# Order of the first loads in a pre-norm attention and feed-forward kernel: activation tiles 4 to 6 ahead of the feed-forward factors, and new planned arrival times

## The chip, the cores and the metric

The kernel runs on the 8 cores of one Trainium2 chip. Each core computes one of the 8 batch elements; the cores exchange nothing. The metric is the device time of the slowest core, in microseconds (us).

## The reference

For each batch element, x has 2048 rows (the sequence) of 1024 features:

```
x = x + Attn(layernorm(x));  x = x + FFN(layernorm(x))
Attn: Q, K, V = h@Wq+bq, h@Wk+bk, h@Wv+bv      16 heads of 64
      scores = Q K^T / 8 + decay,  decay = -0.25*log(i-j) for j < i, 0 for j = i, -inf for j > i
      out = softmax(scores) V @ Wo + bo
FFN:  W_real, W_imag (512 x 512) = einsum('abcd,cefg->abefdg', G1, G2)   (from small factors)
      out_real = xr@W_real.T - xi@W_imag.T + b_real;  out_imag = xr@W_imag.T + xi@W_real.T + b_imag
```

## The kernel before

The 2048 rows are 16 tiles of 128 (a tile number n or t) and 4 chunks of 512 (c). Heads go in 8 pairs (p). TensorE works through numbered groups into two alternating PSUM banks `gp`; a group may start when the group two before it has been evicted. The groups are: T(n), the transposes of a normalised tile (PE line L979); K(c,p) and Q(c,p), the projections of a chunk for one pair, 8 matmuls each (L991); V(t,half), values of a tile for eight heads (L1001); N and B, a bound on the scores from the squared norms of Q and K (L1012, L1020); O and F, the output projection and the feed-forward. The attention proper runs in 320 steps: scores (L1055, L1057) on TensorE, the exponential X on ScalarE (L931), the product with the decay P on VectorE (L798), the values and row sums on TensorE (L1079, L1085). The groups of the second half of a chunk and of the next chunk are laid between the attention steps.

The start of chunk 0 has no attention steps beside it. TensorE's order there is T(0) to T(3), K(0,0) to K(0,3), Q(0,0) to Q(0,3), N(0,0), V(0,0), N(0,1), V(1,0), V(2,0), B(0,0), V(3,0), then the scores of the first two steps, K(0,4), Q(0,4), K(0,5) and so on. Pairs 0 to 3 need the first halves of the weights (columns 0 to 511), pairs 4 to 7 the second halves. In chunk 0 ScalarE evicts K and Q; VectorE evicts N and V. Before N(0,0), VectorE squares Q and K of pairs 0 and 1 (L772, L773), before N(0,1) those of pairs 2 and 3.

GpSimd issues all weight loads at the start, in the order Wk, Wq, Wv first halves, then Wk, Wq, Wv second halves (L604, through the software queue q0). SyncE issues the rest (hardware queue q1): tiles 0 to 3 of x, then behind a wait for Wk's first half half of the V bias `bvB` and the selectors, behind a wait for Wq's first half what the change touches. Tiles 4 and later go to three buffers `xrot`; tile 7 and every later one waits in SyncE's queue until the tile that held its buffer is normalised (L578 to L580).

A tile's layer norm on VectorE is two halves of statistics (S1, S2: L653, L660) and the application A (L670); ScalarE computes the reciprocal root R between them. The 56 factor steps W on VectorE (L755, L759) build the feed-forward weight from `g1s` and `g2s`; after each 7 ScalarE rounds the result (WR, L911, L913). The first W step waits for both loads. `g1s` and `g2s` lie where chunk 2's attention output is written later, so the first normalisation of chunk 2 waits for the last rounding.

TensorE's order does not depend on planned times of loads: `make_fill` writes it from costs and due places. The orders of ScalarE and VectorE are written by `make_orders`: it plays the program with a planned duration for each instruction and a planned arrival time for each load (the tasks with `"dma"`), and, whenever one of the two engines is free, takes among the work that is ready by the plan's clock what TensorE needs soonest. At run time each engine follows this order strictly and waits where the real data are late.

Of the kernel before, what the change touches and what calls it, by code (L numbers as in the profile page):

```python
# [71 lines left out]
def on_act(lab):  # L72

    return (lab[0] == "B" or (lab[0] in ("K", "Q") and lab[1] == 0)
            or (lab[0] == "T" and (lab[1] < 4 or lab[1] >= NT + 12)))
# [129 lines left out]
def make_orders(plan):  # L205
# [9 lines left out]
    def task(engine, key, us, *of):  # L215
        tasks[key] = (engine, us, [k for k in of if k])
# [9 lines left out]
    for k in pe:  # L226
        if k[0] == "S":
            c, p, mt = STEPS[k[1]]
            task("pe", k, (512 - trim(c, mt)) / 2400, k[1] >= 2 and ("X", k[1] - 2), ("E", ("Q", c, p)), ("E", ("K", c, p)))
        elif k[0] == "V":  # L230
            c, p, mt = STEPS[k[1]]
            n = c * PAIRS + p
            task("pe", k, (512 - trim(c, mt)) / 1600 + 0.02, ("P", k[1]), mt == 0 and n and ("Z", n - 1),
                 ("E", ("V", mt, p // 4)))
        else:
            _, lab, k0, k1 = k
            what, n = lab[0], lab[1]
# [5 lines left out]
            us = {"T": 0.06, "N": 0.08, "B": 0.14}.get(what, 0.216) * (k1 - k0)  # L243
            task("pe", k, us, *((of + [bank(groups.index(lab))]) if k0 == 0 else []))
            if k1 == PASSES[what]:
# [16 lines left out]
                us = {"B": 0.3, "T": 0.65}.get(what, 0.67) + (0.4 if what == "T" and on_act(lab) else 0.0)  # L262
# [10 lines left out]
    for n in range(2 * NT):  # L273
        x = [("dma", "x", n)] * 2 if n < NT else [("E", ("O", n - NT, h)) for h in range(2)]
        task("dve", ("S1", n), 0.62, x[0], n and ("S2", n - 1), n >= 4 and ("A", n - 4))
        task("dve", ("S2", n), 0.9, x[1], ("S1", n))
        task("act", ("R", n), 0.6, ("S2", n), n and ("R", n - 1))
        task("dve", ("A", n), 0.75, ("R", n), n and ("A", n - 1), n >= 2 and ("D", ("T", n - 2)))
        if n < NT:
            task("dma", ("dma", "x", n), 7.5 + 1.4 * n if n < 4 else (34.0, 36.0, 44.0)[n - 4] if n < 7 else 5.0, n >= 7 and ("A", n - 3))  # L280
            task("dma", ("dma", "bo", n), 10.0, ("E", ("O", n - 4, 1)) if n >= 4 else ("A", NT - 1))
            task("dma", ("dma", "bf", n), 6.0, ("A", NT + n))
            task("dma", ("dma", "out", n), 4.0, ("E", ("F", n, 1)))
    pairs = [(c, p) for c in range(NCH) for p in range(PAIRS)]
    for i, (c, p) in enumerate(pairs):
        n = c * 4 + p // 2 - 2
# [13 lines left out]
    for i in range(56):  # L300
        task("dve", ("W", i), 0.6, ("W", i - 1) if i else ("dma", "g"), i >= 7 and i % 7 == 0 and ("WR", i // 7 - 1))
        if i % 7 == 6:
            task("act", ("WR", i // 7), 1.4, ("W", i))
    for name, us in (("wka", 20.0), ("wqa", 27.0), ("wva", 39.0), ("wkb", 47.0), ("wqb", 54.0), ("wvb", 61.0), ("g", 33.0)):
        task("dma", ("dma", name), us)


# [53 lines left out]
    while at < len(pe) or could["act"] or could["dve"]:  # L361
# [6 lines left out]
        t, engine = min(starts)  # L368
# [16 lines left out]

PLAN = make_plan()
ACT_ORDER, DVE_ORDER = make_orders(PLAN)
GROUPS = [lab for s in PLAN for lab in s["done"]]
GROUP_AT = {lab: n for n, lab in enumerate(GROUPS)}
# [7 lines left out]
def build_program():  # L397
# [11 lines left out]
    dg1 = nc.dram_tensor("g1t", [512, 256], F32, kind="ExternalInput").ap()  # L409
    dg2 = nc.dram_tensor("g2t", [512, 128], F32, kind="ExternalInput").ap()  # L410
# [3 lines left out]
    with ExitStack() as TOP:  # L414
        E = TOP.enter_context

        def sem(name):
            return E(nc.semaphore(name))
# [8 lines left out]
        s_ident, s_cols, s_sel, s_g = sem("ident_in"), sem("cols_in"), sem("selectors_in"), sem("g_in")  # L427
# [19 lines left out]
        def place(name, cols, dt, at=None, parts=128):  # L447
            size = cols * (4 if dt == F32 else 2)
            if at is None:
                at = (top[0] + 31) // 32 * 32  # L450
                top[0] = at + size
            return nc.alloc_sbuf_tensor_at(name, [parts, cols], dt, offset=at), at
# [33 lines left out]
        g1s, _ = place("g1s", 4 * 256, F32, at=at_attn + 16384)  # L486
        g2s, _ = place("g2s", 4 * 128, F32, at=at_attn + 16384 + 4096)
# [19 lines left out]
        def evicted(lab):  # L507

            return (s_eva if on_act(lab) else s_evd), EVICT_AT[lab]

        def x_tile(n):

            if n < 4:
                return xfirst[:, n * 1024:(n + 1) * 1024], s_x0[n], 16
            j = (n - 4) % 3
            return xrot[:, j * 1024:(j + 1) * 1024], s_xr[j], 16 * ((n - 4) // 3 + 1)

        def res_tile(i):

            return xres[:, :] if i % 4 == 3 else xrot[:, (i % 4) * 1024:(i % 4 + 1) * 1024]  # L520
# [26 lines left out]
        @blk.sync  # L547
        def _(s):
            def load_x(n):
                dst, got, _ = x_tile(n)  # L550
                s.dma_start(out=dst, in_=dx[n * 128:(n + 1) * 128, :]).then_inc(got, 16)

            def load_bv(half):
                s.dma_start(out=bvB[:, half * 512:(half + 1) * 512],
                            in_=dbv[:, half * 512:(half + 1) * 512].partition_broadcast(128)).then_inc(s_bv[half], 16)

            load_x(0)
            load_x(1)
            s.dma_start(out=ident[:, :], in_=dident).then_inc(s_ident, 16)
            load_x(2)  # L560
            load_x(3)
            s.dma_start(out=cols[:, 0:16], in_=dcols[:, 0:16]).then_inc(s_cols, 16)

            s.wait_ge(s_w["wk_a"], 16)
            load_bv(0)
            s.dma_start(out=cols[:, 16:528], in_=dcols[:, 16:528]).then_inc(s_sel, 16)
            s.wait_ge(s_w["wq_a"], 16)
            s.dma_start(out=g1s[:, :].rearrange("p (t n) -> p t n", t=4),
                        in_=dg1.rearrange("(t p) n -> p t n", p=128)).then_inc(s_g, 16)
            s.dma_start(out=g2s[:, :].rearrange("p (t n) -> p t n", t=4),  # L570
                        in_=dg2.rearrange("(t p) n -> p t n", p=128)).then_inc(s_g, 16)
            load_x(4)
            load_x(5)
            s.wait_ge(s_w["wv_a"], 16)
            load_x(6)
            load_bv(1)
            for n in range(7, NT):

                s.wait_ge(s_xn, n - 2)
                load_x(n)  # L580
            for i in range(NT + 4):
                if i < NT:
                    if i < 3:

                        s.wait_ge(s_xn, NT - 2 + i)
                    elif i == 3:

                        s.wait_ge(s_grp, GROUP_AT[("Q", NCH - 1, PAIRS - 1)] + 1)
                    else:
                        s.wait_ge(*evicted(("O", i - 4, 1)))  # L590
                    s.dma_start(out=res_tile(i), in_=dx[i * 128:(i + 1) * 128, :]).then_inc(s_res[i % 4], 16)
                if i >= 4:
                    t = i - 4
                    s.wait_ge(*evicted(("F", t, 1)))
                    s.dma_start(out=dout[t * 128:(t + 1) * 128, :],
                                in_=outb[:, (t % 2) * 1024:(t % 2 + 1) * 1024]).then_inc(s_out[t % 2], 16)
            s.wait_ge(s_out[0], 16 * NT // 2)
            s.wait_ge(s_out[1], 16 * NT // 2)
# [568 lines left out]
```

## Time and profile before

| | |
|---|---|
| median of 3 runs | 615.36 us (615.26 to 615.51) |
| the profiled execution | 614.41 us |
| its span on the slowest core (core 3) | 612.8 us |
| spans of all cores | 607.5 to 612.8 us |
| TensorE busy on core 3 | 532.2 us (87%) |
| VectorE busy | 475.3 us (78%) |
| ScalarE busy | 370.3 us (60%) |
| mean granted clock of TensorE, cores | 0.968 to 0.980 |

The profiled execution is one run, 0.95 us below the median of the timed runs; its span leaves out 1.6 us before the first and after the last instruction. The busy times are those of the slowest core. Busy shares are averages over stages; the stretch that the change touches is the first 70 us.

### The profile page before, as it was taken

What the parts mean: (1) busy time and instruction counts of PE and PEld (TensorE: products, weight loads), DVE (VectorE), ACT (ScalarE), POOL (GpSimd) and SP (SyncE); (2) the same over time, 40 slices, a digit from 0 to 9 for tenths busy, and PEclk for the clock granted to TensorE, in tenths of its full rate; (3) what the DMA queues carried; (4) which work ended last, traced back from release to release, by engine and by line L of the source; (5) the groups of instructions that cost most, each with busy time, mean ns of one, the idle gap of its engine ahead of it and who ended that gap; (6) DMA issues with size and microseconds to landing.
All of it is one profiled execution on the core that took longest, in us unless ns stands there. A gap on an engine that the chain in (4) does not pass through costs nothing.

```text
span 612.8 us, 16752 instructions; the slowest of 8 cores (607.5 to 612.8 us)
## 1 busy us (share of the span) xinstructions
PE 532.2 (87%) x6144; PEld 244.1 (40%) x6144; DVE 475.3 (78%) x840; ACT 370.3 (60%) x508; POOL 36.1 (6%) x44
## 2 busy tenths in 40 slices
PE   1747987979989898999989998889999999999987
PEld 1312333434344344344434444343444444444443
DVE  5417898999999999776777677858788888878682
ACT  2610653557756677675766766747777777777220
POOL 5000000000000000000000020010111110111120
PEclk9985998999999999997999999979999999999999
DMA  8999303100012001002000019773566566656755
GB/s 185 164 203 215 61 2 104 36 2 1 3 41 66 2 3 35 3 2 71 1 3 1 2 18 154 149 132 104 136 141 140 123 139 156 139 128 151 172 103 172
DMA packets 20655, 53.03 MB, mean 87 GB/s; under 512 B 1760, under 2 KB 8928, under 8 KB 20576
## 3 DMA queue, kind: packets, MB, share of 16 engines
q0 software_dynamic: 11888, 25.17, 26.0%
q1 hardware_dynamic: 8688, 26.79, 13.5%
q8 instruction: 52, 0.85, 0.6%
q14 instruction: 27, 0.22, 0.1%
HBM read 51.95 MB, written 8.39 MB: 98 GB/s over the span
## 4 chain that ended last, share of the span: by engine, by line
PE 57%; DVE 14%; DMA 10%; issue 10%; ACT 7%; DVEq 0%; ACTq 0%; SPq 0%; POOL 0%; POOLq 0%
PE gp L991 11%; PE pv L1079 10%; PE stP L1055 9%; PE gp L1031 8%; PE gp L1041 7%; PE gp L1001 5%; ACT PT L931 5%; PE pr L1085 4%; DMA Wq<-wq 4%; DMA Wo<-wo 3%; DMA xrot<-x 3%; DVE PT L798 3%; DVE attnT L815 2%; PE gp L979 1%; DVE stat L660 1%
## 5 line engine op out<-in xcount | busy, mean ns | idle before, releaser
L931 ACT ACTIVATE PT<-stP,negc 128x1024 bf16<-128x1024 f32 (+1 forms) x320 | 301.4, 983 | 141.3 <-PE stP L1057 141.0
L798 DVE TENSOR_TENSOR PT<-PT,decay 128x1024 bf16<-128x1024 bf16 (+1 forms) x320 | 192.0, 606 | 49.2 <-ACT PT L931 47.2
L1079 PE MATMUL pv<-PT,V 128*32 128x256 bf16 (+3 forms) x2560 | 108.3, 262 | 4.7 <-DVE PT L798 3.9
L1055 PE MATMUL stP<-QT,KT 64*128 64x512 bf16 (+1 forms) x320 | 91.0, 354 | 8.5 <-ACT PT L931 8.2
L1057 PE MATMUL stP<-QT,KT 64*128 64x512 bf16 (+1 forms) x320 | 91.4, 355 | 0.0
L1085 PE MATMUL pr<-PT,ones 128*32 128x256 bf16 (+3 forms) x1280 | 84.2, 260 | 0.0
L1001 PE MATMUL gp<-Wv,xnT 128*128 128x512 bf16 x256 | 69.5, 404 | 15.2 <-DVE V L705 8.4
L1079 PEld LDWEIGHTS pv<-PT,V 128*32 128x32 bf16 x2560 | 53.0, 96 | 66.5 <-issue 63.2
L991 PE MATMUL gp<-xnT,Wk 128*128 128x512 bf16 x256 | 67.2, 395 | 4.4 <-DVE xnT L696 1.9
L991 PE MATMUL gp<-xnT,Wq 128*128 128x512 bf16 x256 | 63.8, 380 | 6.1 <-DVE KT L710 4.7
L1031 PE MATMUL gp<-Wo,attnT 128*128 128x512 bf16 x256 | 62.4, 380 | 5.5 <-DVE x L727 2.6
L1041 PE MATMUL gp<-Wf,xn2T 128*128 128x512 bf16 x256 | 62.6, 383 | 2.3 <-DVE outb L736 1.2
L815 DVE TENSOR_TENSOR attnT<-pv,recip 64x512 bf16<-64x512 f32 x64 | 44.0, 687 | 2.8 <-ACT recip L941 1.6
L1001 PEld LDWEIGHTS gp<-Wv,xnT 128*128 128x128 bf16 x256 | 22.6, 102 | 47.8 <-issue 30.4
L1055 PEld LDWEIGHTS stP<-QT,KT 64*128 64x128 bf16 x320 | 20.5, 94 | 52.9 <-issue 52.0
L979 PE MATMUL gp<-ident_s,xnrot 128*128 128x128 bf16 x256 | 24.2, 235 | 19.7 <-DVE xnrot L670 16.1
L991 PEld LDWEIGHTS gp<-xnT,Wq 128*128 128x128 bf16 x256 | 22.9, 97 | 38.7 <-issue 15.7
L991 PEld LDWEIGHTS gp<-xnT,Wk 128*128 128x128 bf16 x256 | 23.1, 100 | 36.9 <-issue 16.1
L1031 PEld LDWEIGHTS gp<-Wo,attnT 128*128 128x128 bf16 x256 | 22.4, 97 | 36.8 <-issue 15.4
L1041 PEld LDWEIGHTS gp<-Wf,xn2T 128*128 128x128 bf16 x256 | 22.6, 98 | 33.1 <-issue 10.2
L1085 PEld LDWEIGHTS pr<-PT,ones 128*32 128x32 bf16 x1280 | 34.9, 98 | 0.9
L859 ACT ACTIVATE stat<-stat,cst 128x1 f32<-128x1 f32 x32 | 9.3, 291 | 39.6 <-DVE stat L662 39.6
(67 smaller groups left out, 452.4 us busy)
## 6 DMA issues: line engine op xcount, KB each, us to landing
xrot<-x SPq DMA_DIRECT2D x24, 512.0 KB, 4.8
x<-bfn POOLq DMA_DIRECT2D x16, 512.0 KB, 5.8
out<-outb SPq DMA_DIRECT2D x16, 512.0 KB, 4.0
xrot<-bo POOLq DMA_DIRECT2D x12, 512.0 KB, 5.7
xfirst<-x SPq DMA_DIRECT2D x4, 512.0 KB, 7.1
Wk<-wk POOLq DMA_DIRECT2D x2, 1024.0 KB, 25.8
Wq<-wq POOLq DMA_DIRECT2D x2, 1024.0 KB, 36.1
Wv<-wv POOLq DMA_DIRECT2D x2, 1024.0 KB, 41.7
```

Of the source, the lines that this page charges most:

```text
L798: v.tensor_mul(pt, pt, decay[:, off + no:off + 512].unsqueeze(1).to_broadcast([128, 2, 512 - no])).then_inc(s_pm, 1)
L815: ins = v.tensor_mul(out, pv[x:x + 64, :].rearrange("p (d m q) -> p d m q", d=2, q=64), recip[x:x + 64, :].rearrange("p (m q) -> p m q", q ...
L931: a.activation(p_tile(g, no), st_tile(g, no), AF.Exp, bias=negc[:, c * 8 + p % 2 * 4 + p // 2:][:, 0:1]).then_inc(s_exp, 1)
L979: ins = t.transpose(ps[:, :].bitcast(BF16)[:, k * 128:(k + 1) * 128], xnrot[:, o + k * 128:o + (k + 1) * 128], ident[:, 0:128])
L991: ins = t.matmul(ps[:, :], W[:, k * D + p * 128:k * D + (p + 1) * 128], xnTv[:, k, :], start=(k == 0), stop=(k == FT - 1))
L1001: ins = t.matmul(ps[:, :], xnTv[:, k, j * 128:(j + 1) * 128], Wv[:, k * D + half * 512:k * D + (half + 1) * 512], start=(k == 0), stop=(k ...
L1031: ins = t.matmul(ps[:, :], attnT[:, o + k * 512:o + k * 512 + 128], Wo[:, k * D + ch * 512:k * D + (ch + 1) * 512], start=(k == 0), stop=( ...
L1041: ins = t.matmul(ps[:, :], xn2Tv[:, i % 2, k], Wf[:, k * D + ch * 512:k * D + (ch + 1) * 512], start=(k == 0), stop=(k == FT - 1))
L1055: t.matmul(stP[g % 2][:, no:512], KT[0:64, ks:ks + 128], QT[0:64, qs + no:qs + 512], start=True, stop=True, tile_position=(0, 0))
L1057: t.matmul(stP[g % 2][:, 512 + no:1024], KT[64:128, ks:ks + 128], QT[64:128, qs + no:qs + 512], start=True, stop=True, tile_position=(64, ...
L1079: t.matmul(pv[x:x + 32, half * 256 + no // 2:(half + 1) * 256], V[:, vo + h * 64 + half * 32:vo + h * 64 + half * 32 + 32], p_part(g, h, a ...
L1085: ins = t.matmul(pr[x:x + 32, no // 2:256], ones32[:, :], p_part(g, h, a, no), start=first, stop=last, tile_position=(0, x), skip_group_ch ...
```

## The change

SyncE issues tiles 4 and 5 directly behind its wait for Wq's first half, tile 6 and the second half of `bvB` directly behind its wait for Wv's first half, and the factors after them, ahead of the waits for later tiles. Before, the factors stood ahead of tiles 4 and 5. In the planning pass the planned arrival times of tiles 4 to 6, of the six weight halves and of the factors are replaced. Nothing else differs; the orders of VectorE and ScalarE follow from the planning pass.

```diff
@@ make_orders
-            task("dma", ("dma", "x", n), 7.5 + 1.4 * n if n < 4 else (34.0, 36.0, 44.0)[n - 4] if n < 7 else 5.0, n >= 7 and ("A", n - 3))
+            task("dma", ("dma", "x", n), 7.5 + 1.4 * n if n < 4 else (37.0, 39.0, 46.0)[n - 4] if n < 7 else 5.0, n >= 7 and ("A", n - 3))
@@ make_orders
-    for name, us in (("wka", 20.0), ("wqa", 27.0), ("wva", 39.0), ("wkb", 47.0), ("wqb", 54.0), ("wvb", 61.0), ("g", 33.0)):
+    for name, us in (("wka", 18.5), ("wqa", 26.0), ("wva", 35.0), ("wkb", 43.0), ("wqb", 50.0), ("wvb", 58.0), ("g", 58.0)):
         task("dma", ("dma", name), us)
@@ blk.sync
             s.wait_ge(s_w["wq_a"], 16)
-            s.dma_start(out=g1s[:, :].rearrange("p (t n) -> p t n", t=4),
-                        in_=dg1.rearrange("(t p) n -> p t n", p=128)).then_inc(s_g, 16)
-            s.dma_start(out=g2s[:, :].rearrange("p (t n) -> p t n", t=4),
-                        in_=dg2.rearrange("(t p) n -> p t n", p=128)).then_inc(s_g, 16)
             load_x(4)
             load_x(5)
             s.wait_ge(s_w["wv_a"], 16)
             load_x(6)
             load_bv(1)
+            s.dma_start(out=g1s[:, :].rearrange("p (t n) -> p t n", t=4),
+                        in_=dg1.rearrange("(t p) n -> p t n", p=128)).then_inc(s_g, 16)
+            s.dma_start(out=g2s[:, :].rearrange("p (t n) -> p t n", t=4),
+                        in_=dg2.rearrange("(t p) n -> p t n", p=128)).then_inc(s_g, 16)
```

## Rows read from the trace of the kernel before

**Rows 1.** Slices of the page (core 3): busy tenths in 40 equal slices.

```profile
PE   1747987979989898999989998889999999999987
DVE  5417898999999999776777677858788888878682
```

**Rows 2.** Spans and mean granted clock of two cores.

```profile
core 3: 612.8 us, clock 0.968
core 4: 609.6 us, clock 0.974
```

**Rows 3.** Timeline of SyncE's issues, core 3: start, duration, line, output<-input, count.

```profile
28.70 0.38 SPq L568 DMA_DIRECT2D g1s<-g1t  x1
...
29.93 5.75 SPq L551 DMA_DIRECT2D xrot<-x  x3
35.73 0.65 SPq L554 DMA_DIRECT2D bvB<-bv  x1
```

**Rows 4.** Tiles Wk and Wq, core 3: issues (first and last start), time to landing.

```profile
L604 POOL DMA_DIRECT2D Wk<-wk x2: 903/984/1065, 6.0 to 8.8; - x2
...
DMA to landing us min/median/max: 12.6/25.8/39.0
...
L604 POOL DMA_DIRECT2D Wq<-wq x2: 914/976/1039, 7.0 to 9.6; - x2
...
DMA to landing us min/median/max: 21.6/36.1/50.6
```

**Rows 5.** DMA issues, core 3, in 0 to 130 and (tile 7) 52 to 53 us: us to landing.

```profile
g2s<-g2t SPq DMA_DIRECT2D x1, 256.0 KB, 15.6
...
xrot<-x SPq DMA_DIRECT2D x1, 512.0 KB, 7.8
```

**Rows 6.** Timeline of TensorE, core 3: start, duration, group [idle before <-releaser].

```profile
30.36 7.07 PE L991 MATMUL gp<-xnT,Wq 128*128 128x512 bf16 x32 [0.28 <-ACT KT L882]
46.44 0.62 PE L1012 MATMUL gp<-sqb,ident_s 128*32 128x512 bf16 x4 [9.01 <-DVE sqb L773]
46.99 3.59 PE L1001 MATMUL gp<-Wv,xnT 128*128 128x512 bf16 x8
...
61.61 1.89 PE L1001 MATMUL gp<-Wv,xnT 128*128 128x512 bf16 x8 [0.32 <-DVE V L705]
63.43 0.39 PE L1055 MATMUL stP<-QT,KT 64*128 64x512 bf16 x1
...
65.65 1.89 PE L991 MATMUL gp<-xnT,Wq 128*128 128x512 bf16 x8
```

**Rows 7.** Timeline of VectorE, core 3: the first factor step and the sixth.

```profile
44.82 0.69 DVE L755 TENSOR_TENSOR wacc<-g1s,g2s 128x512 f32<-128x512 f32 x1 [10.87 <-DMA g2s<-g2t]
...
62.75 0.67 DVE L755 TENSOR_TENSOR wtmp<-g1s,g2s 128x512 f32<-128x512 f32 x1
```

**Rows 8.** DMA queues, core 3, 34 to 40 us: packets, MB, share of 16 engines.

```profile
q0 software_dynamic: 543, 0.55, 65.6%
q1 hardware_dynamic: 544, 0.47, 41.9%
```

**Rows 9.** Windows of core 3 (first two) and core 2 (last): PEclk, DMA share, GB/s end each row.

```profile
42.00:44.00 2.00, 0.00 (x0) 0.00 (x0) 0.00 (x0) 0.00 (x0) 0.00 (x0) 0.50 1.16 249
58.00:60.00 2.00, 2.00 (x9) 0.87 (x8) 1.13 (x2) 0.00 (x0) 0.00 (x0) 0.84 1.10 255
...
46.00:48.00 2.00, 1.43 (x5) 0.38 (x3) 1.90 (x6) 0.50 (x2) 0.00 (x0) 0.78 1.12 260
```

**Rows 10.** Core 4: Wq's issues and landings, and its group Q(0,4) in the timeline.

```profile
L604 POOL DMA_DIRECT2D Wq<-wq x2: 893/908/924, 6.5 to 9.3; - x2
...
DMA to landing us min/median/max: 20.3/37.2/54.0
...
65.56 1.89 PE L991 MATMUL gp<-xnT,Wq 128*128 128x512 bf16 x8
```

**Rows 11.** Window 70 to 250 us of core 3: PE, PEld, DVE, ACT, POOL busy, PEclk, DMA.

```profile
70.00:250.00 180.00, 158.98 (x1914) 73.57 (x1914) 167.76 (x311) 114.20 (x177) 0.00 (x0) 0.98 0.08 25
```

## The prediction

> **What bounds the kernel now.** I read the page's slices first, then the cores, then the first 70 us of the slowest core. The slices are 15.3 us long. In the third (31 to 46 us) TensorE has a 4 and VectorE a 1; from the fifth on TensorE is at 7 to 9 tenths, and VectorE at 8 to 9 until 245 us [rows 1]. The span that counts is core 3's, 612.8 us; core 4, the other one that I follow, has 609.6 [rows 2].
>
> In the first 70 us of core 3 the chain is this. SyncE issues g1s at 28.70, g2s behind it, then tiles 4 and 5 from 29.93, and, when Wv's first half has landed, tile 6 and bvB at 35.73 [rows 3]. g2s lands 15.6 us after its issue (29.12 + 15.6 = 44.7) [rows 5]. VectorE's order has the first factor step (W 0) behind the first square and ahead of the second, so it stands still for 10.87 us, to 44.82 [rows 7]. TensorE has finished Q's first half at 37.43, needs the second square for N(0,0), and idles 9.01 us, to 46.44; its granted clock falls to half in that time (0.50 in 42 to 44 us) and V(0,0) then takes 3.59 us for eight matmuls where the V group at 61.61 takes 1.89. The first scores come at 63.43, Q(0,4), with K(0,4) between them, at 65.65 [rows 6, 9].
>
> **What the change takes away.** With the factors last and planned at 58, no W step stands before the squares. From there I follow the engines with the durations of the trace. N(0,0) at 37.5, V(0,0) when Wv's first half is in: the two x loads, 4 KB packets, now run beside it, so I move its landing from 35.3 to 37.5. V(0,0) 38.2 to 40.0, each further V group 1.7 behind the eviction of the one two before (0.7 and 0.25 us of hand-over): V(3,0) ends near 47.5. Scores at 47.7 instead of 63.43: 15.7 us earlier. Tiles 4 and 5 don't stop VectorE on the way: an x load alone beside the weights takes 7.8 us from issue to landing [rows 5], so tile 4, issued at 28.7, lands at 36.5, tile 5 some 2.3 us later, tile 6 (issued at 37.5) at 45.3, and VectorE comes to their statistics at 39, 43 and 46. What was waited for goes; what is late next is a weight.
>
> **What is late next.** K(0,4) needs Wk's second half, issued at 8.76, landed 39.0 us later, at 47.8. Q(0,4) needs Wq's second half, issued at 9.63, landed at 9.63 + 50.6 = 60.2 [rows 4]. TensorE's order is fixed, nothing can pass Q(0,4). Today the landing is hidden: 65.65 - 60.2 = 5.4 us of slack. The change does not move it much. The DMA engines are full in this stretch (share 1.10 to 1.16 in three windows) [rows 9], and the same transfers stand before the end of Wq's second half in both orders: bvB and the selectors, g1, g2, tiles 4 to 7 and the other half of bvB. From 34 to 40 us the weights' queue got 543 packets and SyncE's 544 [rows 8]: they alternate, so 1024 small packets of the factors and 384 of tiles 4 to 6 cost the weights the same turns whichever comes first. (The Trainium skill, DMA: Bandwidth & Descriptors, Queues, rings and completion order, says that each engine goes round-robin between its rings by packet. The trace agrees, 543 to 544; by that rule reordering inside SyncE's ring brings Wq no earlier, which speaks against most of this change.) I put it at 60.3, with 58 and 62 as ends. Tile 7, issued when tile 4 is normalised, at 43, stands in the ring behind g1 and g2 and lands near 60 to 61, as it does now (52.25 + 7.8), so its statistics and those behind them come no earlier either. g1 and g2, issued at 38 and served behind tile 6 and bvB, are in by 57 to 60: (15.6 us as now, and some 2 and 4 us for the two ahead).
>
> So at Q(0,4) on core 3: 65.65 to 60.4, **-5.2 us**; 10 of the 15.7 us won are lost to a new idle stretch of TensorE, from K(0,4)'s end at some 49.8 to 60.4. On core 4 Wq's second half is issued at 9.3 and lands 54.0 us later, at 63.3, and Q(0,4) starts at 65.56 [rows 10]: **-2.2 us** there.
>
> **The clock in the new idle stretch.** 9.01 us of idleness were followed by half clock today. The new idleness is 10.6 us (core 3) to 14 us (core 4), so I expect half clock before 60, and now what comes behind it is the densest stretch of TensorE's early work (K and Q groups back to back), which runs at full clock today (eight matmuls in 1.7 to 1.9 us). How long it lasts after work has begun: on core 2 work begins at 43.7 and in 46 to 48 the clock is already 0.78 [rows 9], some 3.8 us; core 3 had gaps in its work and got it back only after 58. From 3.8 to 7 us at half clock cost 1.9 to 3.5 us; I take **+2.7**. Ends: 0 (the wait is shorter than I think and the clock stays) and +6 (as long as on core 3 today, 12.9 us, at half).
>
> **The factor steps that come later.** 56 steps of 0.68 us, pitch 0.6, must be done before the first pair of chunk 2 is normalised (its output overwrites the factors' place). Before Q(0,4) six are done today (44.82 to 62.75) [rows 7]. Then none is, and the plan has them only from 58, 8 us of plan time behind Q(0,4) (planned at 50 by Wq's second half), while VectorE has gaps there because K and Q of chunk 0 are evicted by ScalarE. I count 6 steps from before Q(0,4) and 4 from behind it that move into the later stretch: 10 x 0.6 = 6 us of VectorE. From 70 to 250 us VectorE is busy 167.76 of 180 us and TensorE 158.98 [rows 11]: 12.2 us of VectorE's idleness are there to take them up, in small pieces. If all fits, it costs 0; if VectorE is the bound throughout, 6. TensorE's own share is 88%, so it is not pushed one for one: I take a third, **+2.0**. On the other side nothing of x moves later.
>
> The two edits to planned weight times (18.5, 26, 35, 43) move no order on TensorE and come before their users in the plan; I cost them at nothing, and +-1 us for the other order of VectorE and ScalarE, both ways.
>
> **Sum.** Core 3: -5.2 + 2.7 + 2.0 = -0.5, to 612.3. Core 4: -2.2 + 2.7 + 2.0 = +2.5, 609.6 to 612.1. The slowest core is then at 612.3. The profiled execution took 614.41 with a span of 612.8, so 1.6 around it: 613.9, and the median of the runs, 615.36, lies 0.95 above that execution: **614.9 us**, no change that can be told (0.2% is 1.2 us).
>
> **Rivals.**
> *The start is won and kept.* The half clock falls beside evictions and the factor steps fit into VectorE's gaps: both terms 0. Core 3 at 607.6, core 4 at 607.4: -5, 610. For it: VectorE has 12.2 us idle in 70 to 250, and the plan fills gaps with the steps. Against: TensorE waits for VectorE's evictions all through that stretch. 0.20.
> *Wq's second half really lands near the 50 planned.* Then Q(0,4) starts at about 52, no half clock; -13.6 with the +2 and some more for the steps: -10, 605. For it: the planned times of tiles 4 and 5 (37, 39) agree with my 36.5 and 38.8. Against: 60.2 us, a full ring and the equal turns. 0.10.
> *Slower: VectorE is the bound to 250 us.* The place is VectorE between Q(0,4) and the last factor step; each step moved behind Q(0,4) then costs its 0.6, and the factors' own deadline (the first output of chunk 2) adds a wait if they finish late. Core 4: -2.2 + 3.5 + 6 = +7.3, 616.9 against 612.8, +4: 619. It decides once more than about 5 of the steps find no gap. For it: 93% busy. Against: some of the 12.2 us of idleness can be used. 0.22.
> *Terms cancel*, the forecast, 0.48, own range 612.5 to 617: 0.10 of it faster, 0.28 the same, 0.10 slower.
>
> Together: faster 0.10 + 0.20 + 0.10 = 0.40, same 0.28, slower 0.10 + 0.22 = 0.32. Range 608.5 to 619.5: it takes in most of the first and third rival, with Wq's landing at 58 or 62 as its further ends, and leaves out the second.
>
> **What would show it.** Right: VectorE's 10.9 us wait for g2s is gone; scores at 47 to 49; TensorE waits 8 to 13 us on Wq's second half ahead of Q(0,4), which starts at 59 to 62 on core 3 and 63 to 64 on core 4; half clock around 55 to 66; the first W step after 68 and the last after 225. Wrong: Wq's second half at 50 to 55; VectorE stopped at tile 4, 5 or 6 by more than 1 us; the full clock through the wait; the distance from Q(0,4) to the last W step shorter than today's.

## The result, and the profile after

The changed kernel takes 618.99 us (median of 6 runs, 617.58 to 621.33) against 614.77 us of the kernel before in the same runs (613.68 to 615.51): ratio 1.0071, 95% interval 1.0054 to 1.0088. It is **slower by 4.2 us**. The forecast was 614.9, no change to be told; the range 608.5 to 619.5 holds the time, the direction is missed. Now and then an execution of any of these kernels is several per cent longer, with a lower granted clock on the cores of one die; the ratios leave such executions out.

Slices of the page and spans of the two cores that the prediction follows [rows 1, 2]; core 4 is now the slowest, so the slices are its own (before they were core 3's), and the trace rows below are of core 3:

```profile
PE   1775877989889888878988998888999999999987
DVE  5453588999989999976777587767788888878682
```

```profile
core 3: 615.2 us, clock 0.974
core 4: 616.6 us, clock 0.971
```

A slice is 15.4 us. VectorE's third (31 to 46 us), a 1 before, is now a 5; the fourth and fifth (46 to 77 us), 7 and 8 before, are 3 and 5: the empty stretch at the start has not gone but moved back.

TensorE's timeline on core 3 [rows 6]:

```profile
36.48 0.40 PE L1012 MATMUL gp<-sqb,ident_s 128*32 128x512 bf16 x4
40.08 3.13 PE L1001 MATMUL gp<-Wv,xnT 128*128 128x512 bf16 x8 [3.19 <-DMA Wv<-wv]
...
50.81 0.39 PE L1055 MATMUL stP<-QT,KT 64*128 64x512 bf16 x1
...
60.17 3.57 PE L991 MATMUL gp<-xnT,Wq 128*128 128x512 bf16 x8 [6.98 <-DMA Wq<-wq]
...
68.84 1.89 PE L991 MATMUL gp<-xnT,Wq 128*128 128x512 bf16 x8 [2.58 <-ACT QT L888]
```

N(0,0) comes 10 us earlier (36.48 for 46.44), the scores 12.6 us (50.81 for 63.43), Q(0,4) 5.5 us (60.17 for 65.65). Then Q(0,5) waits for an eviction on ScalarE, and only 1.9 us are left (68.84; the kernel before has it at 70.71). VectorE's and ScalarE's timelines show who is behind that:

```profile
65.23 0.69 DVE L653 BATCH_NORM_STATS2 stat<-xrot 128x6 f32<-128x512 f32 x1 [13.47 <-DMA xrot<-x]
...
72.96 0.69 DVE L755 TENSOR_TENSOR wacc<-g1s,g2s 128x512 f32<-128x512 f32 x1
```

```profile
67.53 0.30 ACT L859 ACTIVATE stat<-stat,cst 128x1 f32<-128x1 f32 x1 [13.26 <-DVE stat L662]
67.92 0.21 ACT L862 ACTIVATE stat<-stat 128x1 f32<-128x1 f32 x1
68.03 0.67 ACT L888 ACTIVATE QT<-gp,bq_s 128x512 bf16<-128x512 f32 x1
```

VectorE stands 13.5 us at tile 7's statistics; the reciprocal root of that tile stands ahead of Q(0,4)'s eviction in ScalarE's order, so a matmul group that ended at 63.7 is evicted at 68.03. Tile 7 is planned 5 us after the tile whose buffer it takes, and stands in SyncE's ring behind the factors. Its load (first row, from its issue at 45.46) and g2s, by the DMA issues:

```profile
xrot<-x SPq DMA_DIRECT2D x1, 512.0 KB, 19.7
...
g2s<-g2t SPq DMA_DIRECT2D x1, 256.0 KB, 20.8
```

The decisive place is 190 us further on. Last factor steps, their rounding, the first normalisation of chunk 2 (L815, which divides the attention output by its row sums) and what TensorE does, from the timelines of VectorE, ScalarE and TensorE:

```profile
259.29 0.69 DVE L755 TENSOR_TENSOR wtmp<-g1s,g2s 128x512 f32<-128x512 f32 x1
...
260.78 0.68 DVE L759 TENSOR_TENSOR wacc<-wacc,wtmp 128x512 f32<-128x512 f32 x1
...
263.24 1.38 DVE L815 TENSOR_TENSOR attnT<-pv,recip 64x512 bf16<-64x512 f32 x2
```

```profile
261.56 0.63 ACT L911 ACTIVATE Wf<-wacc 128x512 bf16<-128x512 f32 x1
262.10 0.62 ACT L913 ACTIVATE Wf<-wacc 128x512 bf16<-128x512 f32 x1
```

```profile
264.77 0.40 PE L1079 MATMUL pv<-PT,V 128*32 128x256 bf16 x8 [2.78 <-DVE attnT L815]
...
266.25 3.15 PE L991 MATMUL gp<-xnT,Wk 128*128 128x512 bf16 x7
```

The same place in the kernel before (VectorE, TensorE):

```profile
258.64 1.38 DVE L815 TENSOR_TENSOR attnT<-pv,recip 64x512 bf16<-64x512 f32 x2
```

```profile
261.87 0.40 PE L1079 MATMUL pv<-PT,V 128*32 128x256 bf16 x8
...
263.18 1.68 PE L991 MATMUL gp<-xnT,Wk 128*128 128x512 bf16 x7
```

Before, the last step started at 226.3, 32 us ahead of the normalisation at 258.64, and nothing waited for it. Now it starts at 260.8, and its rounding ends at 262.7. The normalisation may not start before that, and in VectorE's order, planned with that wait, it stands behind the decay products 109 and 110 (counted from 0; before it stood ahead of both). It starts at 263.24, 0.5 us after the rounding, and VectorE itself doesn't stand still ahead of it on any core: the deadline acts through the planned order, and the real one lies only 0.5 us earlier. TensorE waits 2.78 us for it on every core, its granted clock falls to half (0.72 over 264 to 270 us) and the seven matmuls behind take 3.15 us instead of 1.68.

The starts of the 320 decay products (L798) can be compared one by one on the same core of both traces. Core 3 is 2.0 us ahead at the third (index 2), 1.2 ahead at index 96 (the first of chunk 2), 0.9 behind at index 110, 3.0 behind at index 128 and 2.4 behind at the end. The loss between index 110 and 128 is on every core: 2.0, 2.0, 5.1, 2.0, 5.1, 3.6, 3.6 and 3.6 us for cores 0 to 7. It differs because the kernel before has half clock of its own in this stretch, on six of its eight cores. Windows of the stretch, granted clock third from the end: core 3 and core 4 of the kernel before, core 3 of the changed kernel.

```profile
261.70:291.77 30.07, 27.73 (x334) 13.29 (x332) 21.65 (x39) 19.08 (x23) 0.00 (x0) 0.89 0.13 37
263.15:290.12 26.97, 24.64 (x334) 12.23 (x332) 21.70 (x39) 19.03 (x23) 0.00 (x0) 1.00 0.13 41
```

```profile
262.64:294.76 32.12, 27.66 (x332) 12.72 (x332) 23.74 (x44) 19.64 (x26) 0.00 (x0) 0.89 0.12 34
```

Before, the stretch takes 27.0 us where the clock stays full (cores 2 and 4), 28.5 on cores 5 to 7 and 30.1 on cores 0, 1 and 3, where it is half from 280.5 to 287.3 (core 3). In the changed kernel it takes 32.1 us on all eight cores, with half clock twice (265.8 to 269.2 and 286.3 to 289.7 on core 3). So the loss of 5.1 us against a core at full clock is 2.0 us of wait and order (32.1 against 30.1, both with 6.8 us of half clock) and 3.1 us of clock, half of it behind the wait and half 20 us later, where no wait of TensorE is longer than 1.2 us. Another 2.2 us (core 3; 20.8 to 23.0 us) are lost between index 96 and 110, ahead of the wait and at full clock: 8 factor steps fall there now, none did before.

### The profile page after: what moved, and what is told of

It reads as the page before. It is cut to its first block, busy times and chain, and to the rows that moved or that the text cites. A ratio compares the mean times of both kernels' runs of the same rounds, so it can differ in the third digit from the quotient of the medians.

```text
span 616.6 us, 16666 instructions; the slowest of 8 cores (607.8 to 616.6 us)
## 1 busy us (share of the span) xinstructions
PE 522.8 (85%) x6058; PEld 244.4 (40%) x6144; DVE 476.0 (77%) x840; ACT 369.8 (60%) x508; POOL 36.1 (6%) x44
## 4 chain that ended last, share of the span: by engine, by line
PE 55%; DVE 13%; DMA 12%; issue 10%; ACT 8%; DVEq 0%; POOL 0%; ACTq 0%; another core or an unknown queue 0%; POOLq 0%; SPq 0%
PE gp L991 10%; PE pv L1079 10%; PE stP L1055 9%; PE gp L1031 7%; PE gp L1041 7%; ACT PT L931 6%; PE gp L1001 5%; DMA Wv<-wv 5%; PE pr L1085 4%; DMA xrot<-x 3%; DMA Wo<-wo 3%; DVE PT L798 3%; PE gp L979 2%; DVE attnT L815 2%; PE gp L1020 1%
## 5 line engine op out<-in xcount | busy, mean ns | idle before, releaser
L798 DVE TENSOR_TENSOR PT<-PT,decay 128x1024 bf16<-128x1024 bf16 (+1 forms) x320 | 192.0, 605 | 49.3 <-ACT PT L931 47.2
L1001 PE MATMUL gp<-Wv,xnT 128*128 128x512 bf16 x235 | 62.6, 393 | 19.0 <-DVE V L705 5.7
L991 PE MATMUL gp<-xnT,Wq 128*128 128x512 bf16 x243 | 63.9, 396 | 14.7 <-DMA Wq<-wq 6.6
L1031 PE MATMUL gp<-Wo,attnT 128*128 128x512 bf16 x237 | 58.5, 379 | 7.8 <-DVE x L727 2.6
L1041 PE MATMUL gp<-Wf,xn2T 128*128 128x512 bf16 x239 | 59.4, 382 | 4.7 <-issue 1.8
L815 DVE TENSOR_TENSOR attnT<-pv,recip 64x512 bf16<-64x512 f32 x64 | 44.0, 687 | 2.8 <-ACT recip L941 1.6
L1031 PEld LDWEIGHTS gp<-Wo,attnT 128*128 128x128 bf16 x256 | 22.4, 97 | 36.8 <-issue 15.4
```

Of the source, the lines that this page charges most:

```text
L798: v.tensor_mul(pt, pt, decay[:, off + no:off + 512].unsqueeze(1).to_broadcast([128, 2, 512 - no])).then_inc(s_pm, 1)
L815: ins = v.tensor_mul(out, pv[x:x + 64, :].rearrange("p (d m q) -> p d m q", d=2, q=64), recip[x:x + 64, :].rearrange("p (m q) -> p m q", q ...
L991: ins = t.matmul(ps[:, :], W[:, k * D + p * 128:k * D + (p + 1) * 128], xnTv[:, k, :], start=(k == 0), stop=(k == FT - 1))
L1001: ins = t.matmul(ps[:, :], xnTv[:, k, j * 128:(j + 1) * 128], Wv[:, k * D + half * 512:k * D + (half + 1) * 512], start=(k == 0), stop=(k ...
L1031: ins = t.matmul(ps[:, :], attnT[:, o + k * 512:o + k * 512 + 128], Wo[:, k * D + ch * 512:k * D + (ch + 1) * 512], start=(k == 0), stop=( ...
L1041: ins = t.matmul(ps[:, :], xn2Tv[:, i % 2, k], Wf[:, k * D + ch * 512:k * D + (ch + 1) * 512], start=(k == 0), stop=(k == FT - 1))
```

## The experiments

Each was timed against the kernel before on its own chip; the ratios, with their 95% intervals, are what to compare. **Deadline theory**: the factor steps come too late in VectorE's order, and the last holds up chunk 2's first normalisation (in the plan's clock, and so in the order). **Start theory** (the rival): the loss comes from what waits in the first 70 us (tile 7, half clock) and the orders that follow from it.

**1. The new order of loads under the old plan.**

```diff
-(37.0, 39.0, 46.0) ... ("wka", 18.5) ... ("g", 58.0)
+(34.0, 36.0, 44.0) ... ("wka", 20.0) ... ("g", 33.0)
```

> The changed order of the loads with the planned times, and so the engine orders, of before. The first factor step then stands between the first and the second square while its factors are issued at 41 and land at about 62. Both theories: VectorE stops until about 62, N(0,0) starts near 62 instead of 46.4, and everything behind it is late by 13 to 17 us: about 628 to 632. Deadline theory (the loss sits where the last factor steps hold up the first normalisation of chunk 2): no such wait here, the last factor step well before that normalisation, as before. It shows what the planned times are worth when loads are moved.

630.45 us, 1.024 (1.0212 to 1.0268). VectorE's longest wait, as expected:

```profile
DVE wacc L755 <- DMA g2s<-g2t: 24.1, 1, 24.1
```

Core 3 is 14.0 us late at the first decay product and still 13.7 at index 110; the last factor step is at 240, and there is no loss between 110 and 128. Moving a load without its planned time costs what the load is late.

**2. The new plan over the old order of loads.**

```diff
 (before's blk.sync)
-(34.0, 36.0, 44.0) ... ("g", 33.0)
+(37.0, 39.0, 46.0) ... ("g", 58.0)
```

> The planned times, and so the engine orders, of the change with the loads issued as before. Tile 4 lands at 47 and now stands ahead of V(0,0)'s eviction, so the scores start at 55 to 58 and Q(0,4) at 60 to 61 as in the changed kernel, waiting for Wq's second half. Deadline theory: the late factor steps are the same, TensorE waits for the first normalisation of chunk 2 as in the changed kernel, and the time is 617 to 620. Start theory (the loss comes from what waits in the first 70 us, tile 7 behind the factors above all): tile 7 lands at 58 to 60 here instead of 65, and the time is 613 to 616.

619.02 us, 1.0048 (1.0023 to 1.0073), as slow as the whole change within the intervals. Part of the start is won here too (core 3: tile 4's wait first, then Q(0,4)):

```profile
47.96 0.69 DVE L653 BATCH_NORM_STATS2 stat<-xrot 128x6 f32<-128x512 f32 x1 [9.77 <-DMA xrot<-x]
```

```profile
61.74 1.89 PE L991 MATMUL gp<-xnT,Wq 128*128 128x512 bf16 x8 [0.17 <-DMA Wq<-wq]
```

At index 96 six cores are 1.2 to 3.9 us ahead of before and cores 2 and 4 are 1.6 and 0.6 behind, and from 110 to 128 each of the eight loses 1.9 to 5.1 us. Tile 7 is not late (VectorE waits 1.47 us for it), yet the loss is there: for the deadline, against the start theory. The order of the loads is not what costs, or costs little: the two ratios differ by 0.2% and their intervals overlap.

**3 and 4. 8 of the 56 factor steps, in the changed kernel and in the kernel before.**

```diff
-    for i in range(56):
-        task("dve", ("W", i), ...); if i % 7 == 6: task("act", ("WR", i // 7), 1.4, ("W", i))
+    for i in range(8):
+        task("dve", ("W", i), ...); task("act", ("WR", i), 1.4, ("W", i))
-                u, k = divmod(n, 7)
+                u, k = n, 0
-                a.wait_ge(s_wf, 7 * (u + 1))
+                a.wait_ge(s_wf, u + 1)
```

> The changed kernel with 8 of the 56 factor steps (the first product of each unit; the sums of the other products are left out). Deadline theory: the last step is done by 130, no wait at chunk 2, the start's gain stays: 1 to 5 us faster than the same cut of the kernel before, about 604 to 610. Start theory: not faster than the same cut of the kernel before.

> The kernel before with the same 8 of 56 factor steps (the sums of the other products are left out); the partner of the cut of the changed kernel. 48 steps of 0.6 us less on VectorE: if VectorE is the bound between 70 and 245 us, up to 10 us faster than before, 605 to 612; if they only fill its gaps, within 2 us of 614.8.

Changed: 0.9883 (0.9857 to 0.9909). Before: 0.9942 (0.9920 to 0.9964). With the steps out of the way the change is worth -0.6% (0.9883/0.9942), some 3.6 us, with an uncertainty of 2 us; with all steps it costs 0.7%. The second number has its own use: 48 steps, 29 us of VectorE, are worth only 3.6 us (2 to 5). VectorE at 93% in 70 to 250 us [rows 11] is not the bound there; the steps fill its gaps.

**5. TensorE kept busy while it waits for Wq.**

```diff
                         if piece:
+                            if what == "Q" and p == 4:
+                                for r in range(28):
+                                    t.matmul(ps[:, :], Wk[:, 0:128], xnTv[:, 0, :], start=True, stop=True)
                             t.wait_ge(s_w["w" + what.lower() + piece], 16)
```

> The changed kernel with 28 extra matmuls (6.2 us at full clock) between K(0,4) and Q(0,4), whose results Q(0,4) overwrites: they run where TensorE waits 7 us for Wq's second half. Both theories: the granted clock stays full through the wait and behind it, and K(0,5) ends 2 us earlier. Deadline theory: the first normalisation of chunk 2 still waits for the last factor step, whose VectorE queue still stands at tile 7 to 65 us: no more than 1 us faster than the changed kernel (618 to 619). Start theory (half clock behind Q(0,4) is part of the loss): 2 to 3 us faster than the changed kernel, 616 to 617.

619.6 us, 1.0091 (1.0055 to 1.0127): not faster than the changed kernel. The clock part of the expectation was half wrong. Windows of core 3, granted clock third from the end:

```profile
56.00:60.00 4.00, 1.73 (x9) 0.59 (x6) 0.00 (x0) 0.00 (x0) 0.00 (x0) 1.00 1.07 174
60.00:64.00 4.00, 3.02 (x8) 1.09 (x9) 0.00 (x0) 0.00 (x0) 0.00 (x0) 0.59 1.06 241
```

It stayed full to 60 on all cores, where the changed kernel has 0.50 to 0.85, but five cores (3 among them, with 3.25 us of idleness left behind the extra matmuls) fell to half behind it; cores 1, 2 and 6 kept it throughout. The total gained nothing: Q(0,5) waits for tile 7 through ScalarE (it starts at 67.79 on core 3, 1.0 us earlier than in the changed kernel, and tile 7 landed 1.0 us earlier), so half clock behind Q(0,4) was beside the path there. This speaks against the clock as a part of the loss; that it can be nothing at all is not shown, the interval is 4 us wide.

**6. The factors behind tiles 4 and 5, ahead of the wait for Wv.**

```diff
             load_x(4)
             load_x(5)
+            (g1s, g2s)
             s.wait_ge(s_w["wv_a"], 16)
             load_x(6)
             load_bv(1)
-            (g1s, g2s)
-(37.0, 39.0, 46.0) ... ("g", 58.0)
+(37.0, 39.0, 50.0) ... ("g", 48.0)
```

> The changed kernel with the factors behind tiles 4 and 5 but ahead of the wait for Wv's first half, planned at 48, and tile 6 planned at 50. Factors land at about 50 and the first steps run while TensorE waits for Wq. Deadline theory: as many steps are done before Q(0,4) as in the kernel before, no wait at chunk 2, the start's gain stays: 610 to 613. Start theory: 616 or more, since Q(0,4) starts at 60 as in the changed kernel.

614.33 us, 0.9992 (0.9978 to 1.0005). Better than the change by 0.8%, but not the 610 to 613 expected. Only 13 steps have started by 100 us on core 3 (21 in the kernel before, 9 in the changed one), the last at 254, and TensorE's wait for Wq is twice as long, since Wq's second half lands at 64.7 there, not at 60.0:

```profile
64.83 3.57 PE L991 MATMUL gp<-xnT,Wq 128*128 128x512 bf16 x8 [14.44 <-DMA Wq<-wq]
```

**7. The plan told what the trace shows.**

```diff
-("wqa", 26.0), ("wva", 35.0), ("wkb", 43.0), ("wqb", 50.0), ("wvb", 58.0), ("g", 58.0)
+("wqa", 28.5), ("wva", 40.0), ("wkb", 48.0), ("wqb", 60.0), ("wvb", 69.0), ("g", 62.5)
-... if n < 7 else 5.0, n >= 7 and ("A", n - 3)
+... if n < 7 else 24.0 if n == 7 else 21.0 if n == 8 else 5.0, n >= 7 and ("A", n - 3)
```

> The changed kernel with the planned arrivals set to those that its own trace shows on core 3 (Wv 40 and 69, Wk 48, Wq 28.5 and 60, tiles 7 and 8 near 65, factors 62.5). The first factor step then stands right behind Q(0,4) in the order instead of 8 us of plan time behind it. Deadline theory: the last step comes 4 us or more earlier, little or no wait at chunk 2: 613 to 616. Start theory: no change against the changed kernel, 617 to 620.

613.31 us, 0.9978 (0.9962 to 0.9995). Tile 7's statistics now stand behind the first products, and the third decay product of cores 3, 4 and 5 starts 10.6, 6.2 and 6.4 us ahead of before, instead of 2.0, 1.7 and 7.2 in the changed kernel; at index 96 they are still 9.4, 5.9 and 4.8 ahead. Then the late steps take it back (to 5.2 ahead, 0.9 and 1.0 behind, at 128; the stretch from 110 to 128 takes 32.1 us on every core, as in the changed kernel), with the last step at 252.6 on core 3:

```profile
255.08 1.38 DVE L815 TENSOR_TENSOR attnT<-pv,recip 64x512 bf16<-64x512 f32 x2
```

```profile
PE pv L1079 <- DVE attnT L815: 2.8, 1, 2.8
```

So the expectation that no wait would be left was wrong, the time right.

**8. One number: the factors planned at 50 instead of 58.**

```diff
-("g", 58.0)
+("g", 50.0)
```

> The changed kernel with one number changed: the factors planned at 50 instead of 58. They really land at 62 and tile 7 at 65, so nothing can wait longer at the start than it does, but the first step stands 8 us of plan time earlier in VectorE's order. Deadline theory: the last step is done before chunk 2's first normalisation, 611 to 615. Start theory: 617 to 620.

612.87 us, **0.9974** (0.9958 to 0.9989): faster than both kernels, 1.0% better than the changed one by the two ratios. The loads are issued as in the change, VectorE still stands 14.9 us at tile 7, and Q(0,5) still waits behind it (67.56 on core 3, 1.3 us earlier than in the changed kernel, because tile 7 landed 1.2 us earlier in this execution). What the plan moved are the steps: the last one, and the normalisation that now stands clear of it:

```profile
245.77 0.68 DVE L759 TENSOR_TENSOR wacc<-wacc,wtmp 128x512 f32<-128x512 f32 x1
261.06 1.39 DVE L815 TENSOR_TENSOR attnT<-pv,recip 64x512 bf16<-64x512 f32 x2
```

Against the changed kernel's trace, the stretch from index 110 to 128 is 5.1 us shorter on each of the eight cores (5.0 to 5.2):

```profile
263.43:290.43 27.00, 24.66 (x334) 12.21 (x332) 21.70 (x38) 19.05 (x23) 0.00 (x0) 1.00 0.14 41
```

That is the 2.0 us of wait and order and the 3.1 us of clock. It is the run that decides between the theories, with a reserve: the clock stays full here on all eight cores, in the kernel before on two, so a part of what experiment 8 gains on the kernel before is clock. Why it stays full was not tried. How far behind the steps run can be read from the multiplications among them (L755), in windows (length, busy time and count of that line, granted clock, DMA share, GB/s); kernel before, changed kernel, this one:

```profile
40.00:100.00 60.00, 8.23 (x12) 0.86 0.52 112
100.00:170.00 70.00, 6.82 (x10) 0.98 0.06 17
170.00:230.00 60.00, 6.86 (x10) 0.97 0.10 28
230.00:265.00 35.00, 0.00 (x0) 1.00 0.06 17
```

```profile
40.00:100.00 60.00, 4.12 (x6) 0.91 0.52 109
100.00:170.00 70.00, 6.17 (x9) 0.98 0.06 17
170.00:230.00 60.00, 6.84 (x10) 0.97 0.09 28
230.00:265.00 35.00, 4.80 (x7) 1.00 0.06 17
```

```profile
40.00:100.00 60.00, 6.16 (x9) 0.94 0.54 104
230.00:265.00 35.00, 2.40 (x4) 1.00 0.06 17
```

**9. Half the dose: 54.**

```diff
-("g", 58.0)
+("g", 54.0)
```

> The changed kernel with the factors planned at 54, halfway between its 58 and the 50 that took 6 us off. Deadline theory: a dose in between: the last factor step 4 to 10 us earlier than in the changed kernel and the first normalisation of chunk 2 waits less or not: 613 to 617. If the order is simply different by chance in each plan, the time need not lie between 612.9 and 619.

613.49 us, 0.9976 (0.9959 to 0.9994); the last step starts at 248.6 on core 3, the normalisation at 256.3. Not between 58 and 50 but the same as 50: the normalisation either stands behind the last rounding or clear of it.

**10. The honest plan with the factors at 54.**

```diff
-("g", 62.5)
+("g", 54.0)
```

> The plan with the arrivals that the trace shows, but the factors planned at 54 instead of 62.5. With all arrivals told as they are, the first score products came 10 us earlier and the stretch to chunk 2 was won, and then 4 to 5 us were given back at chunk 2's first normalisation, the last factor step being at 252 to 257. Deadline theory: with the steps earlier in the order that gift is kept in part: 609 to 612. Against it: with 54 the first step stands ahead of work that TensorE needs while the factors land at 62: then 614 or more.

615.8 us, 0.9998 (0.9973 to 1.0023): my expectation missed. The last step is at 226.8, no wait at chunk 2, but core 3 has only 1.7 us left at index 2 and is 0.5 behind before from index 12 on. The first step now stands ahead of the squares that TensorE needs and waits for its factors:

```profile
DVE wacc L755 <- DMA g2s<-g2t: 7.1, 1, 7.1
```

**11 and 12. The factor steps on GpSimd**, under the change's plan and under the honest one.

```diff
-        task("dve", ("W", i), 0.6, ...)
+        task("dma", ("W", i), 1.5, ...)
 @blk.gpsimd, behind the weight loads
+            for n in range(56):
+                wf_step(n)        # g.tensor_mul / g.tensor_add in place of v.
```

> The changed kernel with the 56 factor steps on GpSimd, planned at 1.5 us each, out of VectorE's order. Deadline theory: nothing is late at chunk 2 as long as a step takes less than 3.4 us (190 us for 56 steps), and VectorE has 34 us less: 604 to 610 if GpSimd's steps don't slow VectorE; if they take its reads and writes of memory in turn with it, its own instructions get longer while they run and the gain goes, 612 to 620. Start theory: not below 617.

> The same with the factor steps on GpSimd under the plan with the arrivals that the trace shows. Both the start's gain and the room on VectorE: 3 to 6 us faster than the changed order alone with the steps on GpSimd, 600 to 608 unless GpSimd slows VectorE.

634.28 us, 1.0309 (1.0282 to 1.0335), and 622.32 us, 1.0119 (1.0088 to 1.0150). Both misses, by far more than I allowed. Two rows of core 6 of the first (two engines, while GpSimd works through one unit of seven) show why: a product of 128x256 in bf16 takes 1.35 us where it takes 0.283 us in the mean in the changed kernel.

```profile
94.80 1.35 DVE L801 TENSOR_TENSOR PT<-PT,decay 128x256 bf16<-128x256 bf16 x1
```

```profile
94.47 1.53 POOL L638 TENSOR_TENSOR wacc<-wacc,wtmp 128x512 f32<-128x512 f32 x1
```

The honest plan is again better than the change's plan, by 1.8%, and is so without any factor step on VectorE. That is no gain of the start: in the mean of the cores experiment 12 is 0.8 us behind the kernel before at decay product 12, experiment 11 0.4 ahead; the gap opens behind it (at product 80, 8.4 and 20.5 behind), while GpSimd works.

**In one table.** How far the decay products start ahead of the kernel before (us, minus is behind), mean of the eight cores of one execution each:

| | index 2 | 96 | 110 | 128 | last |
|---|---|---|---|---|---|
| the change | 4.0 | 3.6 | 1.6 | -1.8 | -2.8 |
| 1, loads only | -15.2 | -14.7 | -14.7 | -13.6 | -13.5 |
| 2, plan only | 2.7 | 1.7 | -0.3 | -3.7 | -4.3 |
| 3, changed, 8 steps | 3.1 | 5.7 | 5.4 | 6.2 | 6.7 |
| 4, before, 8 steps | 0.1 | 2.5 | 2.2 | 3.0 | 3.4 |
| 5, clock kept | 3.3 | 2.2 | 0.2 | -2.9 | -3.9 |
| 6, factors in the middle | 2.9 | 0.3 | -0.1 | -0.1 | -0.4 |
| 7, plan by the trace | 6.4 | 6.4 | 4.3 | 1.0 | 0.4 |
| 8, factors at 50 | 3.1 | 1.2 | -0.3 | 1.5 | 1.9 |
| 9, factors at 54 | 3.9 | 1.3 | 1.0 | 1.5 | 0.8 |
| 10, plan by the trace, 54 | 1.5 | -1.5 | -1.4 | -0.7 | -0.9 |
| 11, GpSimd | 2.9 | -18.7 | -19.0 | -18.6 | -18.5 |
| 12, GpSimd, plan by the trace | 6.9 | -8.4 | -8.7 | -7.3 | -7.8 |

Wherever the last step is late (the change, 2, 5, 7), 5.1 to 5.4 us go between index 96 and 128; in 8 and 9 nothing goes there, but by index 96 they hold less of the start's gain (1.2 and 1.3 us) than the changed kernel (3.6). Single executions differ: core 3's span is between 609.6 and 618.5 us in six executions of the changed kernel, so a difference of 1 us in one row says nothing.

## Why the prediction was wrong

**The chain at the start: right, in its place if not in every number.** VectorE's 10.9 us wait for g2s is gone; on core 3 the scores came at 50.8 (47.7 foreseen), because Wv's first half landed at 8.0 + 32.0 = 40.0, not 37.5. I had put the two x loads beside its last packets but moved it by 2.2 us only; it was 4.7. Q(0,4) started at 60.17 (60.4 foreseen), and Wq's second half landed at 9.9 + 50.2 = 60.1 (60.3): the equal turns held, from 46 to 60 us the queues got 1312 and 1311 packets:

```profile
q0 software_dynamic: 1312, 1.32, 63.5%
q1 hardware_dynamic: 1311, 1.58, 43.4%
```

That it fits to 0.2 us is luck. What I built on the turns, that the same transfers stand before the end of Wq's second half in both orders, is not so: tile 7 landed ahead of it before (60.1 and 60.2) and lands behind it now (65.1 and 60.0). In the mean of the cores Wq's second half landed at 60.5 before, 58.8 in the changed kernel and 63.1 in experiment 6, so the order inside SyncE's queue moves it by some us both ways. On core 4 it landed at 60.0, not at the 63.3 carried over from the trace of before; the changed kernel's cores lie between 56.6 and 61.2, and the same core differs from one execution to the next.

**The clock: size right, place without effect.** Half clock stood from 57.6 to 64.4 on core 3, as foreseen; Q(0,4) took 3.57 us for 1.89 and the first five matmuls of K(0,5) 1.70 for 1.24, some 2.1 us together. But the +2.7 is not seen on the path: experiment 5 kept the full clock on cores 1, 2 and 6 and the total did not move (within the 4 us of its interval). What held Q(0,5) was tile 7.

**Tile 7: seen, not followed.** I had it landing at 60 to 61, behind the factors; it landed at 65.2, and I did not look up what stood behind its statistics in the orders: the reciprocal root, and behind that Q(0,4)'s eviction. Of 5.5 us at Q(0,4), 1.9 were left at Q(0,5). "On the other side nothing of x moves later" was wrong too: tile 7 landed 5 us later than before on core 3, and 2 us later in the mean of the cores.

**The factor steps: this step failed.** The prediction said "I count 6 steps from before Q(0,4) and 4 from behind it that move into the later stretch: 10 x 0.6 = 6 us of VectorE", and priced them at +2.0 by how full VectorE is. The count was good: by 80 us 15 steps had started on core 3 before, 4 now. The price was sought in the wrong place. Experiment 4 shows that 48 steps together are worth 3.6 us, so ten would cost under 1 us by crowding. What they have is an end date. The trace of before had all that was needed to work it out: the last step 32 us ahead of the normalisation that needs it, and in mid-run a step every 3.3 us (28 started by 140 us, 43 by 190). Eleven steps behind at that rate is 36 us, more than the 32 of slack; even the ten of the prediction give 33. The measured last step moved by 34.5. Instead of +2.0 spread over the whole stretch, 5.4 us went between decay products 96 and 128 in the mean of the cores: 3.4 at the wait and behind it, and 2.0 ahead of it, where eight of the late steps now fall together (whether these 2.0 are their crowding was not tried). The slower rival named this deadline ("adds a wait if they finish late") but hung its price on a busy VectorE, and no slack was subtracted; the forecast's own last line of signs, "the last after 225", would have passed 260 as a success.

**The rivals.** "Wq near 50" did not happen. "The start is won and kept" is what experiments 3 and 8 show in parts: with the deadline out of the way the change gives 0.6% without most of the steps and, with the factors planned at 50, 0.3% (a part of it by the clock that stays full there). The slower side came true through its second clause. That its 619 is the measured time is luck: it is added up from a VectorE that is full and 3.5 us of clock at the start, and neither was found on the path.

**The sum as measured on core 3** (span 612.8 to 615.2): -2.0 at the third product, +0.8 to index 96, +2.2 to index 110 (where late steps fall), +2.0 to index 128 (the wait; the half clock of the kernel before on this core cancels the changed kernel's), -0.6 to the end: +2.4. On core 4, which has the full clock there before, the same two stretches cost 1.8 and 5.1, and that made it the slowest.

**Open.** The 2.0 us of wait and 3.1 us of clock at the deadline are read from the traces; no experiment took them apart. What the steps cost between index 96 and 110 is read from the change, 2 and 7 only; experiment 8 loses 1.5 us there with one step in the stretch on core 3. Why the honest plan with factors at 54 gives up the start, beyond the 7.1 us wait for g2s, is not settled; nor whether a plan exists that keeps the 9 us of experiment 7 on core 3 and meets the deadline. Taking the factors out of chunk 2's output space was not tried.

## What to carry to other kernels

Work that fills gaps has no price per piece but an end date: when it is moved back by k pieces, multiply by the time between two pieces in mid-run and compare with the slack between its last piece and the instruction that needs it. A planned arrival in a static scheduler is a position in a queue, not a fact: the factors really land at 62, and 58 was worse than 54 or 50, because VectorE waited for something later still anyway. Where it did not (experiment 10), the early position cost a wait of 7.1 us. And when a load is moved behind others, follow every later load of that ring too, with all that stands behind its first reader on any engine.

## What the runs showed of the hardware that was not expected

VectorE is held up while GpSimd works through the factor steps, by more than I allowed. In experiment 11 a decay product of 128x1024 on core 6, between 70 and 200 us, took 1038 ns in the mean; the changed kernel has 685 there (core 4). A product of 128x256 took 520 for 283. Over all its instructions that is some 27 us more of VectorE between 70 and 200 us. VectorE's evictions from PSUM (688 ns for V, 690 in the changed kernel) were not slower:

```profile
L801 DVE TENSOR_TENSOR PT<-PT,decay 128x1024 bf16<-128x1024 bf16 x22 | 22.4, 1038 | 7.5 <-ACT PT L932 7.5
...
L730 DVE TENSOR_TENSOR V<-gp,bvB 128x512 bf16<-128x512 f32 x9 | 6.2, 688 | 5.7 <-remote 3.3 <-PE gp L1002 2.2
```

What grew were the bf16 products and squares, which read two tensors of on-chip memory (SBUF) and write one, and the normalised tiles, which read one and write one (1595 ns for 807); VectorE's fp32 statistics, which read one and write six numbers a row, stayed as they were (677 and 678 ns, 686 in the changed kernel). GpSimd's own sums took 1.26 to 1.53 us in the first units; whether VectorE causes the longer ones was not tried.
